# Selective-scan stage of a GNN + LSTM kernel: B broadcasts half a state ahead and across the chunk seam, output stage one slot later, step-size sums and a remainder on GpSimd

## The reference

```python
# block 1: graph convolution, then a Mamba layer (state size 16, inner width 256)
h  = relu(adj @ layernorm(x) @ gcn_w + gcn_b);  h = norm(h) * ln_g + ln_b
xc, z = split(h @ w_in);  u = silu(causal_conv4(xc));  dbc = u @ w_xp
dt = softplus(dbc[:, :8] @ w_dt + b_dt);  B = dbc[:, 8:24];  C = dbc[:, 24:]
hst_t = exp(dt_t * A) * hst_{t-1} + dt_t * u_t * B_t        # 8192 steps, 256 x 16 states
y = (hst . C + u * D_skip) * silu(z);  x = x + y @ w_out
# block 2: LSTM over the 8192 tokens of layernorm(x), then prefix and suffix sums; x = x + ...
```

## Time and profile before

| | |
|---|---|
| median of 3 runs | 1697.73 us |
| the profiled execution's own time | 1698.79 us |
| its span | 1696.9 us |
| busy over the span: TensorE, VectorE, ScalarE, GpSimd | 92%, 87%, 59%, 61% |
| first dbu of the scan to the first of k = 16 | 138.64 to 1250.10 us |
| k = 16, k = 17 | 1250.10 to 1336.58, to 1404.45 us |

### The profile page before, as it was taken

How to read it: one execution, slowest core, us unless ns; L and a number is a source line. 1 busy time by engine, 2 the same in 40 slices (tenths; PEclk the granted TensorE clock), 3 DMA queues, 4 the chain that set the end, 5 groups by cost and what they waited for, 6 DMA issues and landing times. The chain is left out here.

```text
span 1696.9 us, 21136 instructions
## 1 busy us (share of the span) xinstructions
PE 1556.1 (92%) x5282; PEld 791.8 (47%) x5282; DVE 1482.2 (87%) x1687; ACT 1005.5 (59%) x2093; POOL 1041.3 (61%) x471
## 2 busy tenths in 40 slices
PE   6999999999999999999999999999977677999994
PEld 2444344444444434343444444444422225999993
DVE  8416999999999999999999999999996995557998
ACT  2244666667575757576666667575757554555552
POOL 4024788887878778878788787878885651001221
PEclk9999999999999999999999999999988899999997
DMA  8976665757566666665665757566610202000002
GB/s 311 343 253 236 229 213 196 255 169 272 197 241 224 215 242 205 235 214 213 224 229 187 257 171 269 203 237 230 209 47 0 94 6 106 0 0 1 0 0 99
DMA packets 52073, 298.31 MB, mean 176 GB/s; under 512 B 5522, under 2 KB 5522, under 8 KB 19092
## 3 DMA queue, kind: packets, MB, share of 16 engines
q1 hardware_dynamic: 49680, 293.30, 48.8%
q10 hardware_dynamic: 2308, 4.20, 0.6%
HBM read 285.68 MB, written 11.80 MB: 175 GB/s over the span
## 5 line engine op out<-in xcount | busy, mean ns | idle before, releaser
L509 PE MATMUL bank<-ring,xh 128*128 128x512 f32 x2048 | 953.1, 593 | 15.5 <-DVE xh L989 15.0
L890 POOL TENSOR_TENSOR work<-work 128x1024 f32<-128x1024 f32 x210 | 516.6, 2460 | 238.3 <-DVE work L1081 232.0
L1123 DVE TENSOR_TENSOR_SCAN work<-bank,hstate,work 128x512 f32<-128x512 f32 x512 | 627.2, 1266 | 2.7 <-ACT bank L760 1.3
L509 PEld LDWEIGHTS bank<-ring,xh 128*128 128x128 f32 x2048 | 388.4, 190 | 458.3 <-issue 422.3
L760 ACT ACTIVATE bank<-work,a_neg 128x512 f32<-128x512 f32 x512 | 345.6, 688 | 306.2 <-DVE work L1123 305.9
L1073 DVE TENSOR_TENSOR work<-work,bank 128x1024 f32<-128x1024 f32 x256 | 309.5, 1214 | 60.0 <-PE bank L446 46.3
L446 PE MATMUL bank<-bc_parts,sel 96*128 96x512 bf16 x512 | 192.9, 385 | 33.3 <-DVE work L1081 25.8
L1081 DVE TENSOR_TENSOR work<-work,bank 128x1024 f32<-128x1024 f32 x182 | 216.2, 1194 | 0.0
L441 PE MATMUL bank<-work,w_sb 128*128 128x512 f32 (+2 forms) x352 | 183.5, 618 | 25.4 <-ACT work L676 11.2
L951 POOL TENSOR_TENSOR work<-work 128x256 f32 x32 | 28.5, 891 | 235.9 <-ACT work L797 235.9
L853 POOL TENSOR_TENSOR work<-work 128x1024 f32<-128x1024 f32 x48 | 113.3, 2361 | 79.9 <-ACT work L658 79.7
(11 more groups left out here) (148 smaller groups left out, 1581.4 us busy)
## 6 DMA issues: line engine op xcount, KB each, us to landing
ring<-adj_t SPq DMA_DIRECT2D x256, 1024.0 KB, 4.8
xh<-x_rows SPq DMA_DIRECT2D x16, 256.0 KB, 6.7
work<-x_t SPq DMA_DIRECT2D x16, 256.0 KB, 4.8
x_scratch<-work ACTq DMA_DIRECT2D x16, 256.0 KB, 5.4
work<-x_scratch SPq DMA_DIRECT2D x1, 4096.0 KB, 13.6
out_t<-work SPq DMA_DIRECT2D x16, 256.0 KB, 2.7
xl_scratch<-work SPq DMA_DIRECT2D x13, 256.0 KB, 2.2
ring<-xl_scratch SPq DMA_DIRECT2D x1, 3328.0 KB, 13.1
```

Of the source, the lines that this page charges most:

```text
L509: last = nc.tensor.matmul(mixed[:, :], xn[:, j, :], a, start=(j == 0), stop=(j == BLK - 1))
L890: nc.gpsimd.tensor_tensor(out=acc, in0=hc[0] if n == 1 else acc, in1=hc[n % 2], op=ALU.add).then_inc(y_added, 1)
L1123: nc.vector.tensor_tensor_scan(hb[s % 2][:, h, :], da[h], dbu[s % 2][:, h, :], hstate[:, HV * s + h:HV * s + h + 1], ALU.mult, ALU.add).th ...
```

## The change

- TensorE: b(s+2) is issued in the middle of slot s, after c(s). In the middle of slots 14 and 15 it issues b(0) and b(1) of the next chunk, after waits for `low_ready` and `mid_ready`.
- Output stage: pcen and pvar go from 12.5 and 13.5 to 13.5 and 14.5; VectorE's L1019 from slot 12 to 13, ahead of L1033 in the same slot; ScalarE's parts from 13 and 14 to 14 and 15; xl from before add(15) to behind it.
- Step-size sums: in the order `wa = wa - wb`, `dt = wa + wd`, on GpSimd in all chunks (the last one too), each ahead of the add of its slot; dtu in slot 13, behind add(12).
- The remainder r1 on GpSimd in slot 10, ahead of add(9), instead of VectorE.

```diff
 SHARED = [...
-          ("out", 11.5, "post"), ("pcen", 12.5, "post"), ("pvar", 13.5, "post")]
+          ("out", 11.5, "post"), ("pcen", 13.5, "post"), ("pvar", 14.5, "post")]
...
-                def spread(bank_, ready, row, n):
+                def spread(bank_, ready, row, n, rows=bc_parts[par]):
...
-                def spread_b(n):
-                    wait(pe, dbu_done, DS * cs + (n - 1))
-                    spread(b_bank, b_ready, n, n)
+                def spread_b(s):
+                    if s < DS - 2 and scan:
+                        wait(pe, dbu_done, DS * cs + (s + 1))
+                        spread(b_bank, b_ready, s + 2, s)
+                    if s >= DS - 2 and pre:
+                        n = s - (DS - 2)
+                        if n == 0:
+                            pe.wait_ge(low_ready, k)
+                            pe.wait_ge(mid_ready, k)
+                        wait(pe, dbu_done, DS * (k - 1) + (n - 1))
+                        spread(b_bank, b_ready, n, n, bc_parts[1 - par])
...
                 def mid_slot(s):
                     shared_steps(s, 0.5)
                     if scan and s > 0:
                         spread_c(s)
+                    spread_b(s)
...
-                    if scan and s == 0:
-                        pe.wait_ge(low_ready, cs + 1)
-                        pe.wait_ge(mid_ready, cs + 1)
-                        spread_b(0)
-                    if scan and s < DS - 1:
-                        spread_b(s + 1)
...
-                    if s == 13:
+                    if s == 14:
                         act.wait_ge(shared_read, shared_index("out", k, pre, post) + 1)
...
-                    if s == 14:
+                    if s == 15:
                         written("pvar")
...
                 def pre_part(s):
-                    if drains(k):
-                        return
+                    if s == 10:
+                        pool.wait_ge(high_ready, k)
+                        nc.gpsimd.tensor_tensor(out=r1[0:PARTS * BC, :], in0=dbc[0:PARTS * BC, :], in1=bc_parts[q][:, :],
+                                                op=ALU.subtract).then_inc(r1_ready, 1)
                     if s == 12:
-                        pool.wait_ge(log_dt, k)
+                        pool.wait_ge(pos_dt, HV * k)
                         pool.wait_ge(rem_dt, k)
-                        nc.gpsimd.tensor_tensor(out=wb, in0=wd, in1=wb, op=ALU.subtract).then_inc(sum_dt, 1)
+                        nc.gpsimd.tensor_tensor(out=wa, in0=wa, in1=wb, op=ALU.subtract).then_inc(sum_dt, 1)
                     if s == 13:
                         pool.wait_ge(sum_dt, k)
-                        pool.wait_ge(pos_dt, HV * k)
-                        nc.gpsimd.tensor_tensor(out=dt[q], in0=wa, in1=wb, op=ALU.add).then_inc(dt_ready, 1)
-                    if s == 14:
-                        pool.wait_ge(dt_ready, k)
-                        nc.gpsimd.tensor_tensor(out=dtu[q], in0=dt[q], in1=u[q], op=ALU.mult).then_inc(dtu_ready, 1)
+                        pool.wait_ge(log_dt, k)
+                        nc.gpsimd.tensor_tensor(out=dt[q], in0=wa, in1=wd, op=ALU.add).then_inc(dt_ready, 1)
+
+                def make_dtu():
+                    pool.wait_ge(dt_ready, k)
+                    nc.gpsimd.tensor_tensor(out=dtu[q], in0=dt[q], in1=u[q], op=ALU.mult).then_inc(dtu_ready, 1)
...
-                    if s == 15 and not (isinstance(k, int) and k == NC + 2):
-                        make_xl(pool, nc.gpsimd, k)
...
+                    if pre:
+                        pre_part(planned(k, s, "pre"))
                     if scan and drains(k):
                         make_hc(s)
                     elif scan and s >= 2:
                         add(s - 1)
-                    if pre:
-                        pre_part(s)
-                    if post and s > 0:
-                        post_part(planned(k, s, "post"))
+                    if pre and planned(k, s, "pre") == 13:
+                        make_dtu()
                 if scan and not drains(k):
                     add(DS - 1)
+                if post and not (isinstance(k, int) and k == NC + 2):
+                    make_xl(pool, nc.gpsimd, k)
...
-                        if pre and s in (12, 13, 14):
-                            make_dt(s)
-                    if post and t == 12:
+                    if post and t == 13:
                         written("out")
...
-                    if pre and s == 10:
-                        dve.wait_ge(high_ready, k)
-                        nc.vector.tensor_tensor(out=r1[0:PARTS * BC, :], ...).then_inc(r1_ready, 1)
-                    if pre and s == 12 and not drains(k):
+                    if pre and s == 12:
                         dve.wait_ge(one_dt, k)
```

More of the change, by code:

```diff
@@ L442, in shared_step @@
                     last.then_inc(shared_written, 1)
-                def spread(bank_, ready, row, n):
+                def spread(bank_, ready, row, n, rows=bc_parts[par]):
                     nc.tensor.matmul(bank_[n % 2][:, :], sel[:, row * P:(row + 1) * P],
-                                     bc_parts[par][:, :], start=True, stop=True).then_inc(ready, 1)
+                                     rows[:, :], start=True, stop=True).then_inc(ready, 1)
                 def spread_c(n):
@@ L1022, in side_part @@
                         nc.vector.tensor_tensor(out=ht, in0=ht, in1=shared[:, :], op=ALU.mult).then_inc(shared_read, 1)
-                    if pre and s == 10:
-                        dve.wait_ge(high_ready, k)
-                        nc.vector.tensor_tensor(out=r1[0:PARTS * BC, :], in0=dbc[0:PARTS * BC, :], in1=bc_parts[q][:, :],
-                                                op=ALU.subtract).then_inc(r1_ready, 1)
-                    if pre and s == 12 and not drains(k):
+                    if pre and s == 12:
                         dve.wait_ge(one_dt, k)
@@ L1049, in finish_y @@
                     nc.vector.tensor_tensor(out=by_step(yp), in0=by_token(yv), in1=by_token(sz[q]), op=ALU.mult).then_inc(y_ready, 1)
-                def make_dt(s):
-                    if s == 12:
-                        dve.wait_ge(log_dt, k)
-                        nc.vector.scalar_tensor_tensor(out=wb, in0=wc, scalar=-1.0, in1=wb, op0=ALU.add,
-                                                       op1=ALU.subtract).then_inc(rem_dt, 1)
-                        dve.wait_ge(rem_dt, k)
-                        nc.vector.tensor_tensor(out=wb, in0=wd, in1=wb, op=ALU.subtract).then_inc(sum_dt, 1)
-                    if s == 13:
-                        dve.wait_ge(sum_dt, k)
-                        dve.wait_ge(pos_dt, HV * k)
-                        nc.vector.tensor_tensor(out=dt[q], in0=wa, in1=wb, op=ALU.add).then_inc(dt_ready, 1)
-                    if s == 14:
-                        dve.wait_ge(dt_ready, k)
-                        nc.vector.tensor_tensor(out=dtu[q], in0=dt[q], in1=u[q], op=ALU.mult).then_inc(dtu_ready, 1)
                 def both(ap):
```

## The result

The changed kernel is slower: a median of 1728.37 us (1723.21 to 1729.65, 4 runs) against 1698.09 (1697.0 to 1702.46, 4 runs), a ratio of the means of 1.0168, 95% interval 1.014 to 1.0195. The profiled execution took 1723.21 us, with a span of 1721.4; before it was 1698.79 and 1696.9, so the two traces differ by 24.4 us and the medians by 30. The forecast was 1717 in a range of 1683 to 1727. The side is right, and so are the two collisions that the forecast rests on. The median lies 11 us above the forecast and 1.4 us above the upper end of the range; the profiled execution lies inside it.

A forecast was written before the change was run, and what follows sets the result against it. VectorE sets the pace, TensorE right under it. Loop +26, k = 2 -3, k = 3 +1.5, k = 16 -4, k = 17 -1 sum to +19.5 on 1698.79: 1718.3, as a median 1717 us, range 1683 to 1727.

The forecast's parts named there:

- the two collisions: VectorE's correction waits behind GpSimd's add(10), its low part behind add(11) (+1.85 us per chunk), for the shared SBUF ports.
- b half a slot ahead: TensorE's earlier b(7) removes VectorE's 1.64 us wait before dbu(7) without adding TensorE work.
- its terms: k = 16: r1, three sums and b waits leave VectorE, later operations meet GpSimd's hc; -4 us, bounds 0 and -8.
- asking at 670.85, comes 0.4 too late: The correction asks for the ports 0.4 us after add(10) starts at 670.45, so ends at 673.9 instead of 674.4.
- the rival that ends faster: The correction asks before add(10), making 14 chunks 2.35 us shorter each: 1717 - 33 = 1684 us; chance 0.22.
- The term of -3: k = 2: earlier first scan, no b wait, r1 off VectorE, correction loses to add(10); 3 us shorter in all.
- Its first scan comes 1.3 sooner: k = 2: the first scan starts 1.3 us sooner, since b(0) and b(1) skip waiting for adj's end.
- the b wait ... go: k = 2: VectorE's wait for b and its r1 operation both vanish, within the -3 us for that chunk.
- some 2 to 3 us, in which it isn't late for anything of VectorE's: TensorE waits 2 to 3 us for ScalarE around the later pcen and pvar, without delaying VectorE.
- what I took off the sum on its way to a median: The summed 1718.3 us for the profiled execution became 1717, the median of the runs being 1.1 us lower.
- xl behind add(15): At the seam xl and adj piece 2 come 1.2 us later; z1 is 0.25 us later in even chunks, loss 0.8 in odd.

The follow-up runs named there:

- e4: The kernel before with only the new order of the b broadcasts (half a slot ahead and across the seam): 1669.26 us, ratio 0.983.
- e1: The changed kernel with VectorE's low part (L1032) ahead of the output stage's residual in slot 13: 1699.97 us, ratio 1.0014 to the kernel before.
- e2: The changed kernel with GpSimd's add(10) one slot later, behind the first step-size sum: 1694.59 us, ratio 0.9979 to the kernel before.
- f5: The changed kernel with the output stage (residual, pcen, pvar) back in its old slots: 1693.96 us, ratio 0.9974 to the kernel before.
- e3: The changed kernel with both edits, low part ahead of the residual and add(10) one slot later: 1670.33 us, ratio 0.9836 to the kernel before.
- f6: The changed kernel with low part first, add(10) later and xl back ahead of add(15): 1659.05 us, ratio 0.9769 to the kernel before.
- f8: The changed kernel with r1 alone back on VectorE, in slot 10: 1714.01 us, ratio 1.0105 to the kernel before.
- g1: The changed kernel with xl alone back ahead of add(15): 1721.46 us, ratio 1.0141 to the kernel before.

## Why the prediction was right, and what it missed

**Right, step by step.** b half a slot ahead takes the wait before dbu(7), 1.64 to 0.23 in the even chunk that the forecast worked out. r1 takes 1.16 us on GpSimd (1.24 was used). L1028 comes behind add(10) and L1032 behind add(11), the latter for 1.74 us a chunk (1.85). Counted from seam to seam, as the forecast did, k = 8 and k = 9 take 81.7 and 81.6 us (predicted: 81.8 and 81.5), and all chunks of the loop but k = 6 lie between 81.6 and 82.6. The loop costs 29.2 us against 26; k = 3, 16 and 17 come within 1.1 us each. For k = 16 that doesn't show that its terms were right: e4, with r1 and the three sums still on VectorE, is 5.4 us shorter there. e1 and e2 took the two collisions out one at a time and each gave at least what the sum had for it.

The loser of a meeting starts its work when the other's instruction is over: L1028 ends 1.1 us behind add(10), wherever in the add it asks (0.12 us in: 3.32 in all; 1.37 in, in f5: 2.08). That is the exclusive lock of "SBUF — State Buffer" in the Trainium skill (section "SBUF: two separate sides"), and the traces here agree with it.

**The margin at add(10).** The step "asking at 670.85, comes 0.4 too late" was right in sign and mis-sized: it was 0.12 us in k = 8 and -0.06 in k = 6. So the rival that ends faster, for which 0.22 stood, did happen, in one chunk of fourteen; with margins of this size its chance could not have been told from the trace of before. That the other thirteen chunks came out as forecast was in this sense partly luck. That it would be worth 33 us over all chunks was right: e2 gave 34.

**k = 2.** The term of -3 was mis-sized; it came to -0.4. "Its first scan comes 1.3 sooner" was about right: the first scan came 0.8 us sooner and from the third state on VectorE was 1.3 ahead. The step that failed is "the b wait ... go". The wait before dbu(7) did go from 1.79 to 0.59, but scan(6) ahead of it now waited 1.11 us for `da`, so the lead was 1.30 behind dbu(7) as it had been ahead of it. r1 then brought 1.6, and the wait for `da` at scan(11) and an L1028 of 3.18 instead of 2.42 took back nearly all: at dbu(13) the lead was 0.32. It is 2.6 us of the error. The same happens at scan(6) in k = 4 and the odd chunks of the loop (0.92 in k = 9). What holds `da` back there was not taken apart.

**The term that was missing.** The sum had pvar's wait, "some 2 to 3 us, in which it isn't late for anything of VectorE's". The wait is there, 2.90. But at its end the clock granted to TensorE fell to 1.2 GHz in 8 of 13 chunks. Where the wait was 1.70 us or less (e2, e1, e3, f6, the kernel before, k = 6 of the kernel after) it fell in none; at 2.62 to 2.67 (f8, k = 4 to 15) in 8 of 12, and not at 2.43 in its k = 3; at 2.82 to 2.91 with xl first (g1) in all 12. This holds for k = 3 to 15. From k = 16 on, where TensorE has much less to do, the clock falls in every trace. What a fall costs is only bounded here. The pvar pair alone is 0.95 us longer (2.08 against 1.13), 3.4 us at half the clock put TensorE at most 1.7 us back, and the chunks with a fall are between 1 us shorter (k = 15) and 1.8 us longer (k = 11) than the nearest ones without. e1 and e2 leave 2.4 and 3.1 us of their loops for the longer wait and its seven falls together. No run changed the wait alone, so this is not shown by an experiment. Why a wait of 2.90 us is followed by a fall in k = 4 and not in k = 8 stays open.

**The 11.4 us of error, in sum.** 4.9 lie in the profiled execution (1723.21 against 1718.3): k = 2 with 2.6, the loop with 3.2, the rest with -0.9. 5.2 lie between it and the median of the four runs, which goes with their lower clock. 1.3 is what I took off the sum on its way to a median. In e1 and e2, where the clock did not fall in the loop, the gain was 5 us larger than expected each; the missing term fits that in sign and size, which is not a proof.

**xl behind add(15).** I had it late by 0.25 us in an even chunk and 0.8 in an odd one, 6 x 0.25 + 6 x 0.8 = 6.3 over the loop. g1 has 7 us for it by the medians, but only 2.6 of the loop in the traces, so whether the size was right stays open.

## What to carry to other kernels

Where VectorE and GpSimd share their SBUF ports, put the VectorE operation with both inputs in SBUF directly behind the one that makes GpSimd's next input: here 0.6 us of another operation in between cost 28 us over the kernel. Work moved to an idle GpSimd pushes all its later work, and whether that pays is decided by which operation stands at the ports when VectorE asks; write the two timelines side by side before and after the move, and distrust a margin under half a microsecond. When a change with a good part in it comes out slower, try the parts alone and then their order: the early broadcasts by themselves were worth 29 us here, r1 on GpSimd between -14 and 17 depending on its neighbours, and three swaps of neighbours turned 1728 us into 1659.

## What the runs showed of the hardware that was not expected

TensorE's clock stood at 2.4 GHz through the loop of the kernel before. In the loops of three others (f8, after, g1) it fell to 1.2 GHz, mostly for 3.4 us, about the end of idle stretches of 2.6 to 2.9 us, in some chunks and not in others. In no loop did it fall behind those of 1.70 us or less. And the two engines' contest for the ports is decided to within the resolution of the trace: 0.06 us ahead, L1028 takes 1.23 us; 0.12 behind, 3.32.
